# A fused two-layer transformer kernel: attention output, norm and first routing moved by batch into the stages around them

## The chip, the cores and the metric

The kernel runs on one core of a Trainium2 chip. The metric is the device time of one execution in microseconds (us), as the median of several executions. The core has five engines that run side by side: TensorE (PE) for matmuls and transposes, VectorE (DVE), ScalarE (ACT), GpSimd (POOL) and SyncE (SP), which here issues nearly all DMAs. They meet only through semaphores.

## The reference, cut to what matters

```
x = L0_attn_x                                   # 4 batches, 1024 tokens, width 128
x = x + attn(layernorm(x)) @ wo                 # 16 heads of 8, mask by pages of 32
xn = layernorm(x)
scores = softmax(xn @ gate_w.T)                 # 8 experts
weights, idx = top_k(scores, 2)
y = sum over e of (x2_e * x3_e * (idx == e))    # experts on xn * weight
x = x + y + silu(xn @ sw1.T) * (xn @ sw2.T) @ sw3.T
x = x + mamba(layernorm(x));  x = x + second_moe(layernorm(x))
```

The attention divides by its softmax sums, multiplies with `wo`, adds to x, normalizes, and a router picks two of eight experts for every token. That part, between the attention and the expert layer, is what the change moves.

## The kernel before, in words

The 4096 tokens are 8 chunks of 512, two to a batch. `X` stays in SBUF as [128 tokens, 32 tiles, 128]; `xnT` is its normalized transpose.

**Attention** (`attend`) runs 16 groups `i` of 4 heads; groups 0 to 3 are batch 0, and so on. A group has 9 steps `k`, a step two pairs. For a pair PE first computes one item of row maxima (`maxima`, L694) that lies 26 items ahead, then scores (L716), then values (L735) of an earlier step. DVE reduces the maxima (L622, 18 a group), ACT takes the exponentials (L670, 36 a group) and stores a group's output (`store`, L659), which SP writes to DRAM (`heads`, L539). POOL negates the next group's maxima (`negate`, L589 to L594); at step 7 PE turns them (`turn`, L702), ACT copies them, SP copies them into the rows of `qr` (L545), and the next group's scores wait for that DMA. SP also loads the rows of the group three ahead: 18 DMAs (L496, L491) at the start of each group up to the 13th. Maxima items end in group 14 (counted from 0), at its step 4. PSUM banks 0 to 3 hold maxima, 4 to 6 scores, 7 values.

**`attention_out`** loads numerators and inverse sums of 8 chunks (4 DMAs of 256 KB a batch, L816 and L817), divides on DVE (L841), multiplies with `wo` on PE (L878), adds to X and takes statistics on DVE (L846, L85). **`norm_transpose`** computes mean and 1/std (seven small DVE steps, POOL's power, L134), normalizes (DVE, L164), turns (PE, L177), copies (ACT, L209) and computes the router's logits (PE, L183). **`route_first`** does softmax and top two in 19 small dependent DVE steps over all 32 tiles at once, turns gates and masks, and writes them to DRAM.

**`first_ffn`** takes one chunk at a time, a Fori over 4 pairs of chunks. For expert e: SP broadcasts a gate row (L1020) and a mask row (L1023) into rings of four; POOL multiplies (`xm`, L1035, three ahead) and accumulates (L1046); PE does `up`, `third` and `second(e-1)`, two 512-column matmuls each (L1147, L1151, L1156); ACT the silu (L1059); DVE `x3s` (L1087) and `product(e-1)` (L1097). In the next chunk PE's `finish` (24 matmuls, L1138 and L1139) closes the chunk.

```
sp.wait_ge(xm_ready, q - ROW_RING + 1)          # before gate row q
pe.wait_ge(prod_ready, 2 + NE * c + e)          # second(e): product(e-1) is done
pe.wait_ge(exp_done, unit - 1)                  # scores: three banks, two written
```

Each stage is a block of its own: all engines meet at its end.

Of the kernel before, what the change touches and what calls it, by code (L numbers as in the profile page):

```python
# [9 lines left out]
F32 = mybir.dt.float32  # L10
BF16 = mybir.dt.bfloat16
# [4 lines left out]
P = 128  # L16
# [401 lines left out]
EARLY = (B - 1) * H  # L418
# [42 lines left out]
TURN_K = 7  # L461
PIECE = 256
# [37 lines left out]
def attend(nc, g):  # L500

    with ExitStack() as ctx:
# [13 lines left out]
        sums = sb("sums", [2 * EARLY, CH])  # L516
        zero_set, ones_set, bottom_set = sem("zero_set"), sem("ones_set"), sem("bottom_set")
        sums_in, inverted, inverse_out = sem("sums_in"), sem("inverted"), sem("inverse_out")
# [3 lines left out]
        out_written = [sem(f"out_written{k}") for k in range(2)]  # L522
# [13 lines left out]
        def _(sp):  # L536
# [15 lines left out]
            for i in range(NG):  # L552
                if i >= 1 and i + RING - 1 < NG:
                    sp.wait_ge(scores_done, UNITS * i)
                    for n in range(ROW_DMAS):
                        load_rows(sp, g, i + RING - 1, n)
                if i >= 1:
                    store(i - 1)
                if i == NG - 1:

                    for k in range(2):
                        sp.wait_ge(out_written[k], 16 * (EARLY // GH // 2))
                    sp.dma_start(sums[:, :], g.heads[0:EARLY, :, D, :]).then_inc(sums_in, 16)
                    sp.wait_ge(inverted, 1)
                    sp.dma_start(g.inverses[0:EARLY, :, :].rearrange("i a (k t) -> i (a k) t", k=CPB), sums[:, :]).then_inc(inverse_out, 16)
                else:
                    neg_in_rows(i + 1)
            store(NG - 1)
            for k in range(2):
                sp.wait_ge(out_written[k], 16 * NG // 2)  # L570
            sp.wait_ge(inverse_out, 16)

        @block.gpsimd
        def _(pool):
# [30 lines left out]
            for i in range(NG - 1):  # L605
                if i >= 1:
                    pool.wait_ge(values_done, NV * i)
                value_columns(i + 1)
                negate(i + 1)

        @block.vector
        def _(dve):
# [28 lines left out]
            dve.wait_ge(sums_in, 16)  # L641
            dve.reciprocal(sums[:, :], sums[:, :]).then_inc(inverted, 1)

        @block.scalar
        def _(act):
# [16 lines left out]
            for i in range(NG):  # L662
                for k in range(NK):
# [3 lines left out]
                    for h in range(GH):  # L667
# [6 lines left out]
                        if k == TURN_K and h == 0 and i < NG - 1:  # L674
                            turned(i + 1)
            store(NG - 1)

        @block.tensor
        def _(pe):
# [63 lines left out]
            for i in range(NG):  # L743
                for k in range(NK):
                    for pair in range(GP):
# [25 lines left out]
def top_two(eng, steps, s, rank, tmp, w1, mask):  # L771


    def over(t):
        return t.rearrange("p (n a) -> p n a", a=1).to_broadcast([P, NT, NE])
    ranks = rank.rearrange("p (a e) -> p a e", a=1).to_broadcast([P, NT, NE])
    steps.done(eng.tensor_reduce(w1[:, :], s[:, :, :], AX.X, ALU.max))
    steps.done(eng.tensor_tensor(tmp[:, :, :], s[:, :, :], over(w1[:, :]), ALU.is_equal))
    steps.done(eng.tensor_tensor(tmp[:, :, :], tmp[:, :, :], ranks, ALU.mult))
    steps.done(eng.tensor_reduce(w1[:, :], tmp[:, :, :], AX.X, ALU.max))  # L780
    steps.done(eng.tensor_tensor(mask[:, :, :], ranks, over(w1[:, :]), ALU.is_equal))

    steps.done(eng.scalar_tensor_tensor(tmp[:, :, :], mask[:, :, :], -4.0, s[:, :, :], ALU.mult, ALU.add))
    steps.done(eng.tensor_reduce(w1[:, :], tmp[:, :, :], AX.X, ALU.max))
    steps.done(eng.tensor_tensor(tmp[:, :, :], tmp[:, :, :], over(w1[:, :]), ALU.is_equal))
    steps.done(eng.tensor_tensor(tmp[:, :, :], tmp[:, :, :], ranks, ALU.mult))
    steps.done(eng.tensor_reduce(w1[:, :], tmp[:, :, :], AX.X, ALU.max))
    steps.done(eng.tensor_tensor(tmp[:, :, :], ranks, over(w1[:, :]), ALU.is_equal))
    steps.done(eng.tensor_tensor(mask[:, :, :], mask[:, :, :], tmp[:, :, :], ALU.add))


def attention_out(nc, g, e):

    with ExitStack() as ctx:
        sb = lambda name, shape, dt=F32: ctx.enter_context(nc.sbuf_tensor(f"ao_{name}", shape, dt))
        sem = lambda name: ctx.enter_context(nc.semaphore(f"ao_{name}"))
        X, PS = g.X, g.PS
        wo = sb("wo", [P, E])
        inverse = sb("inverse", [2 * H, CH])
        num, inv = sb("num", [P, 2, CH]), sb("inv", [P, 2, CH])  # L800
        headT = sb("headT", [P, 2, CH])
        w_in, sums_in, inverted, inverse_out, divided, added, mixed, stats_ready = map(sem, (
            "w_in", "sums_in", "inverted", "inverse_out", "divided", "added", "mixed", "stats_ready"))
        heads_in = [sem(f"heads_in{k}") for k in range(2)]
        block = ctx.enter_context(nc.Block())

        @block.sync
        def _(sp):
            sp.sem_inc(divided, 2)
            sp.dma_start(wo[:, :], g.w["wo"]).then_inc(w_in, 16)  # L810

            def load(b):
                for k in range(CPB):
                    sp.wait_ge(divided, CPB * b + k + 1)
                    heads, tokens = bass.ds(b * H, H), slice(k * CH, (k + 1) * CH)
                    sp.dma_start(num[:, k, :], g.heads[heads, k, 0:D, :]).then_inc(heads_in[k], 16)  # L816
                    sp.dma_start(inv[:, k, :], g.inverses[heads, :, tokens].to_broadcast([H, D, CH])).then_inc(heads_in[k], 16)  # L817

            load(0)
            sp.dma_start(inverse[:, :], g.heads[EARLY:, :, D, :]).then_inc(sums_in, 16)  # L820
            with sp.Fori(1, B - 1) as b:
                load(b)
            sp.wait_ge(inverse_out, 16)
            load(B - 1)
            for dst, src in e.pairs:
                sp.dma_start(dst, src).then_inc(e.loaded, 16)

        @block.scalar
        def _(act):
            for dst, src in e.route.pairs:  # L830
                act.dma_start(dst, src).then_inc(e.route.loaded, 16)
            act.wait_ge(inverted, 1)
            act.dma_start(g.inverses[EARLY:, :, :].rearrange("i a (k t) -> i (a k) t", k=CPB), inverse[:, :]).then_inc(inverse_out, 16)
        @block.vector
        def _(dve):
            dve.sem_inc(mixed, 2)

            def divide(b, k, c):
                dve.wait_ge(heads_in[k], 32 * (b + 1))
                dve.wait_ge(mixed, c + 1)  # L840
                dve.tensor_tensor(headT[:, k, :], num[:, k, :], inv[:, k, :], ALU.mult).then_inc(divided, 1)  # L841

            def add(c, k):
                dve.wait_ge(mixed, 2 + c + 1)
                x = X[:, bass.ds(c * TPC, TPC), :]
                dve.tensor_tensor(x, x, PS[:, k, :].rearrange("p (j e) -> p j e", e=E), ALU.add).then_inc(added, 1)  # L846

            def stats(c):
                dve.wait_ge(added, 2 + c + 1)
                for j in range(TPC):  # L850
                    last = tile_stats(dve, g, c * TPC + j)
                last.then_inc(stats_ready, 1)

            divide(0, 0, 0)
            divide(0, 1, 1)
            dve.wait_ge(sums_in, 16)
            dve.reciprocal(inverse[:, :], inverse[:, :]).then_inc(inverted, 1)
            with dve.Fori(0, B - 1) as b:
                for k in range(CPB):
                    add(CPB * b + k, k)  # L860
                    divide(b + 1, k, CPB * (b + 1) + k)
                    stats(CPB * b + k)
            for k in range(CPB):
                add(NCH - CPB + k, k)
                stats(NCH - CPB + k)
            dve.wait_ge(stats_ready, NCH)

        @block.tensor
        def _(pe):
            pe.wait_ge(w_in, 16)  # L870
            pe.sem_inc(added, 2)
            with pe.Fori(0, B) as b:
                for k in range(CPB):
                    c = CPB * b + k
                    pe.wait_ge(divided, 2 + c + 1)
                    pe.wait_ge(added, c + 1)
                    for j in range(TPC):
# [1114 lines left out]
```

## Time and profile before

| what | value |
|---|---|
| time of three runs | median 1487.25 us (1486.56 to 1489.18) |
| profiled execution | 1483.77 us, its span 1482.0 us |
| busy in the span | PE 82%, DVE 76%, ACT 45%, POOL 44% |
| granted TensorE clock, mean | 0.903 of full |
| attention, from the first exponential to the last | 125.4 to 473.0 us |
| from the last attention output copy to the first matmul of the expert layer | 474.2 to 546.1 us |
| expert layer, first matmul to last add | 546.1 to 772.0 us |

Times in rows count from the start of the span. Idle time of an engine matters only where it sets the end of a stage.

### The profile page before, as it was taken

The numbers are of one execution on the slowest core, as the hardware profiler recorded it, in microseconds if no ns is written. First come the engines' busy times: TensorE is split into PE (matmuls) and PEld (weight loads), VectorE is DVE, ScalarE is ACT, GpSimd is POOL, SyncE is SP. The second block draws the span as 40 slices with busy tenths as digits, with TensorE's granted clock in tenths as the row PEclk, the third lists the DMA queues.
The fourth block names the chain that finished last, engine by engine and source line by source line (L and its number), as shares of the span: only waits on it lengthen the run. The fifth ranks groups of instructions, "written<-read, shape, count | busy, mean of one in ns | idle before, by whom it ended". The sixth has DMA issues, their size and how long they took to land. (4 is left out here: it accounts for less than half of the span.)

```text
span 1482.0 us, 21932 instructions
## 1 busy us (share of the span) xinstructions
PE 1214.9 (82%) x7478; PEld 558.0 (38%) x7478; DVE 1132.8 (76%) x1294; ACT 669.5 (45%) x1046; POOL 645.6 (44%) x464
## 2 busy tenths in 40 slices
PE   4937999999996659999978767877877867766998
PEld 2412334334332544454444212322322322355565
DVE  5868999999990734545556889999999999964554
ACT  2515999999997022222225783333333323302221
POOL 2320000101010206766743068988989989921000
PEclk9956999999999559999997868999999999995999
DMA  4321111111101526334520013432333323400421
GB/s 105 120 94 43 58 49 50 61 47 54 54 17 43 157 40 134 127 106 119 121 51 18 5 52 128 127 128 103 115 122 128 128 98 118 125 8 26 68 57 43
DMA packets 74478, 120.31 MB, mean 81 GB/s; under 512 B 13150, under 2 KB 41638, under 8 KB 74390
## 3 DMA queue, kind: packets, MB, share of 16 engines
q1 hardware_dynamic: 74054, 119.08, 27.5%
q8 instruction: 53, 0.87, 0.2%
q14 instruction: 35, 0.29, 0.1%
q10 hardware_dynamic: 336, 0.07, 0.0%
HBM read 105.09 MB, written 13.63 MB: 80 GB/s over the span
## 5 line engine op out<-in xcount | busy, mean ns | idle before, releaser
L622 DVE TENSOR_REDUCE att_found<-PS 128x2 f32<-128x1024 f32 (+2 forms) x288 | 333.1, 1218 | 10.7 <-PE PS L694 8.8
L1518 PE MATMUL PS<-ms_ch,ident_sb 128*128 128x512 f32 x512 | 269.0, 651 | 72.4 <-POOL ms_ch L1625 72.4
L670 ACT ACTIVATE att_prob<-PS 128x512 f32<-128x512 f32 x576 | 313.4, 596 | 28.4 <-PE PS L716 15.3
L1625 POOL TENSOR_TENSOR ms_ch<-xnT,ms_c_rows 128x1024 f32<-128x1024 f32 x128 | 304.8, 2392 | 41.1 <-DVE xnT L1583 21.6
L1583 DVE TENSOR_TENSOR_SCAN xnT<-ms_decay,PS 128x1024 f32<-128x1024 f32 x96 | 216.0, 2275 | 4.2
L735 PE MATMUL PS<-att_prob,att_v 128*32 128x256 f32 (+1 forms) x2560 | 181.8, 370 | 3.0 <-ACT att_out L659 2.8
L1518 PEld LDWEIGHTS PS<-ms_ch,ident_sb 128*128 128x128 f32 x512 | 98.5, 203 | 194.6 <-POOL ms_ch L1625 107.5
L1556 ACT ACTIVATE PS<-m_dt,m_a 128x1024 f32<-128x1024 f32 x32 | 35.8, 1118 | 260.3 <-DVE xnT L1583 260.3
L694 PE MATMUL PS<-kr,qr 55*128 55x128 bf16 (+4 forms) x1152 | 120.8, 290 | 29.8 <-PEq L260 16.0
L716 PE MATMUL PS<-qr,kr 55*128 55x128 bf16 (+4 forms) x1152 | 114.1, 275 | 14.7 <-ACT att_prob L670 8.2
L1570 DVE TENSOR_TENSOR PS<-ms_dtu,PS 128x1024 f32<-128x1024 f32 x96 | 114.6, 1212 | 6.7 <-PE PS L1509 6.5
L1553 ACT ACTIVATE ms_decay<-m_dt,m_a 128x1024 f32<-128x1024 f32 x96 | 106.2, 1138 | 13.3 <-DVE xnT L1583 13.3
L1087 DVE SCALAR_TENSOR_TENSOR f_x3s<-PS,e_w_b,f_mask_row 128x512 f32<-128x512 f32 x64 | 48.0, 751 | 76.3 <-PE PS L1151 76.2
L1059 ACT ACTIVATE f_h<-PS,e_w_b 128x512 f32<-128x512 f32 x64 | 44.0, 687 | 132.3 <-PE PS L1147 132.3
L1035 POOL TENSOR_TENSOR f_xm<-xnT,f_gate_row 128x512 f32<-128x512 f32 x64 | 81.2, 1270 | 44.0 <-DMA f_gate_row<-gate_rows_dram 41.1
L1046 POOL TENSOR_TENSOR f_yT<-f_yT,f_prod 128x512 f32<-128x512 f32 x56 | 70.9, 1266 | 58.0 <-DVE f_prod L1097 55.5
L1509 PE MATMUL PS<-m_bc,m_w_sel_b 96*128 96x512 bf16 x192 | 63.9, 418 | 33.9 <-DVE xnT L1583 25.2
L694 PEld LDWEIGHTS PS<-kr,qr 48*128 48x128 bf16 (+1 forms) x1152 | 39.6, 97 | 135.5 <-issue 93.0
L134 POOL TENSOR_TENSOR norm_rstd<-norm_tmp,half 128x4 f32<-128x4 f32 x32 | 32.1, 1041 | 110.1 <-DVE norm_tmp L155 110.1
L599 POOL COPY att_v<-V 128x256 f32<-128x256 f32 x32 | 11.8, 398 | 156.3 <-PE PS L735 156.1
L735 PEld LDWEIGHTS PS<-att_prob,att_v 128*32 128x32 f32 x2560 | 54.7, 108 | 62.3 <-issue 53.6
L1632 POOL TENSOR_TENSOR ms_x_row<-ms_dtu,ms_b_row 128x1024 f32<-128x1024 f32 x32 | 75.1, 2348 | 1.8 <-DMA ms_b_row<-bc_rows_dram 1.8
(194 smaller groups left out, 1705.8 us busy)
## 6 DMA issues: line engine op xcount, KB each, us to landing
ms_c_rows<-bc_rows_dram SPq DMA_DIRECT2D x64, 512.0 KB, 5.9
f_gate_row<-gate_rows_dram SPq DMA_DIRECT2D x64, 256.0 KB, 3.5
ms_b_row<-bc_rows_dram SPq DMA_DIRECT2D x32, 512.0 KB, 3.6
f_mask_row<-mask_rows_dram SPq DMA_DIRECT2D x64, 128.0 KB, 3.1
qk_parts_dram<-qkv_parts SPq DMA_DIRECT2D x48, 128.0 KB, 1.8
heads_dram<-att_out SPq DMA_DIRECT2D x16, 256.0 KB, 2.6
f_mask_row<-mask_rows_dram SPq DMA_DIRECT2D x64, 64.0 KB, 3.3
qr<-qk_parts_dram SPq DMA_DIRECT2D x32, 96.0 KB
```

Of the source, the lines that this page charges most:

```text
L622: dve.tensor_reduce(found[:, :, pair, first:first + (n - 1) * step + 1:step], PS[:, bank:bank + 2, :].rearrange("p r (w n) -> p r w n", w= ...
L670: act.activation(prob[:, step % PROB_RING * GH + h, :], PS[:, SCORE_BANK + unit % SCORE_RING, :], ACT.Exp, scale=float(D) ** -0.5).then_in ...
L694: last = pe.matmul(PS[:, MAX_BANK + 2 * (m % 2) + r, at:at + n], rows(qr, count, i, pair, r, q_block * P, P), rows(kr, count, i, pair, r, ...
L716: last[r] = pe.matmul(PS[:, SCORE_BANK + (unit + r) % SCORE_RING, col:col + w], rows(kr, count, i, pair, r, j * P, P), rows(qr, count, i, ...
L735: last = pe.matmul(PS[VW * h:VW * (h + 1), VALUE_BANK, q - half * CH:q - half * CH + w], v1[:, i % 2, half, h, j, :], prob[:, step % PROB_ ...
L1035: pool.tensor_tensor(xm[:, e % XM_RING, :], xnT[:, c * CH:(c + 1) * CH], gate_row[:, e % ROW_RING, :], ALU.mult).then_inc(xm_ready, 1)
L1518: last = pe.matmul(PS[:, Y_BANK + 2 * half + q, :], g.ident[:, :], ch[:, half, q * CH:(q + 1) * CH], start=j == 0 and not odd, stop=j == J ...
L1553: act.activation(decay[:, 2 * odd + half, :], m.dt[:, half, sequence(b)], ACT.Exp, scale=m.a[:, half, n + odd:n + odd + 1]).then_inc(decay ...
L1570: dve.tensor_tensor(inputs(half), dtu[:, half, :], inputs(half), ALU.mult).then_inc(input_ready, 1)
L1583: dve.tensor_tensor_scan(h[:, odd, half, :], factor, x, 0.0, ALU.mult, ALU.add).then_inc(scanned, 1)
L1625: pool.tensor_tensor(ch[:, half, :], h[:, odd, half, :], c_rows[:, s % C_RING, :], ALU.mult).then_inc(ch_ready, 1)
L1632: pool.tensor_tensor(x_row[:, :], dtu[:, 1, :], b_row[:, :], ALU.mult).then_inc(x_row_ready, 1)
```

## The change

The blocks `attention_out`, the norm in front of the expert layer and `route_first` disappear. A class `Front` holds their work as small pieces with fixed places, for each batch b of 1024 tokens.

```
LOADS_AT = 6
SUMS_AT, INVERT_AT, INVERSES_AT, HEADS_AT = (5, 9, 13), (8, 12), (8, 12), (10, 14)

# SP, attention group i
+                if i == LOADS_AT:
+                    sp.dma_start(f.wo[:, :], g.w["wo"]).then_inc(f.wo_in, 16)
+                    for group in (f.e.route, f.e):
+                        for dst, src in group.pairs:
+                            sp.dma_start(dst, src).then_inc(group.loaded, 16)
...
+                for b in range(EARLY):
+                    if i == INVERSES_AT[b]:
+                        f.store_inverses(sp, b)
+                    if i == HEADS_AT[b]:
+                        f.load_heads(sp, b)
# POOL, after value_columns(i + 1) and negate(i + 1)
+                for b in range(EARLY):
+                    if i + 1 == HEADS_AT[b]:
+                        for k in range(CPB):
+                            f.divide(pool, b, k)
+            for b in range(EARLY):
+                f.root(pool, b)
# DVE, before the maxima item m
+                for b in range(EARLY):
+                    if m == NI * INVERT_AT[b]:
+                        f.invert(dve, b)
# ACT, after step k
+                    if i == NG - 1 and k in (0, 4):
+                        for part in range(CPB):
+                            f.store_x(act, k // 4, part)
+                    if i == NG - 1 and k in (2, 6):
+                        f.exp(act, k // 4)
+                    if i == NG - 1 and k == 7:
+                        f.store_rows(act, 0)
# PE, after step k
+                    if i == NG - 2 and k in (6, 7):
+                        pe.wait_ge(max_taken, NG * NI)
+                        for part in range(CPB):
+                            f.mix(pe, k - 6, part)
+                    if (i, k) == (NG - 2, 8) or (i, k) == (NG - 1, 3):
+                        for part in range(CPB):
+                            f.turn_x(pe, k // 8 ^ 1, part)
+                    if i == NG - 1 and k in (1, 5):
+                        f.logits(pe, k // 4)
+                    if i == NG - 1 and k == 6:
+                        f.turn_rows(pe, 0)
...
+            f.turn_rows(pe, 1)
```

After its last maxima item DVE does `invert(2)`, then for batch 0 `add` (with statistics), `moments` (seven steps), `normalize`, for batch 1 `add`, and so on to the 19 routing steps of each batch. In the expert layer, now written out for all 8 chunks instead of a loop, batches 2 and 3 are placed at pairs (chunk, expert):

```
# SP: after the mask row of (0, 3): load_heads(2), load_sums(3); (1, 1) store_inverses(3); (1, 4) load_heads(3)
#     (3, 7) store_row_tables(2); (6, 0) store_row_tables(3)
# POOL, at the end of the turn of e (which begins with gated(e + 3)):
+                    if c == 0 and e in (1, 2):
+                        f.divide(pool, 2, e - 1)
+                    if (c, e) == (0, 6):
+                        f.root(pool, 2)
# PE, after second(e - 1)
+                    for b, at, part in ((2, (0, 3), 0), (2, (0, 4), 1), (3, (2, 7), 0), (3, (3, 1), 1)):
+                        if (c, e) == at:
+                            f.mix(pe, b, part)
+                    for b, at, part in ((2, (1, 1), 0), (2, (1, 2), 1), (3, (3, 5), 0), (3, (3, 6), 1)):
+                        if (c, e) == at:
+                            f.turn_x(pe, b, part)
# DVE, after product(e - 1)
+                for b, at, part in ((2, (0, 7), 0), (2, (1, 1), 1), (3, (3, 5), 0), (3, (3, 6), 1)):
+                    if (c, e) == at:
+                        f.normalize(dve, b, part)
# ACT
+                    for b, at in ((2, (1, 6)), (3, (4, 3))):
+                        if (c, e) == at:
+                            act.preload_act_table(ACT.Exp)
+                            f.exp(act, b)
+                            act.preload_act_table(ACT.Silu)
```

The other pieces of batches 2 and 3 are placed in the same way (DVE: `invert(3)` at (0, 2), `add(2)` at (0, 4) and (0, 5), `moments(2)` at (0, 6); PE: `logits` at (1, 4) and (4, 1), `turn_rows` at (2, 7) and (5, 2)). Two of the new functions:

```
    def load_heads(self, sp, b):
        sp.wait_ge(self.inverse_out, 16 * (b + 1))
        if b > 0:
            sp.wait_ge(self.divided, CPB * b)
        for k in range(CPB):
            sp.dma_start(self.num[:, k, :], ...).then_inc(self.heads_in[k], 16)
            sp.dma_start(self.inv[:, k, :], ...).then_inc(self.heads_in[k], 16)

    def divide(self, pool, b, k):
        pool.wait_ge(self.heads_in[k], 32 * (b + 1))
        ...
        pool.tensor_tensor(self.headT[...], self.num[:, k, :], self.inv[:, k, :], ALU.mult).then_inc(self.divided, 1)
```

The division moves from DVE to POOL. A chunk's `mix` or `turn_x` is four fp32 products of 128 columns, 8 matmul instructions; a batch's `logits` is 16.

## Rows read from the trace of the kernel before

**Rows 1.** Stretches: length; busy PE, PEld, DVE, ACT, POOL; clock, DMA share, GB/s.
```profile
441.00:475.00 34.00, 28.33 (x413) 10.38 (x409) 5.47 (x5) 31.26 (x59) 1.25 (x5) 1.00 0.07 22
...
508.00:532.00 24.00, 20.17 (x96) 19.64 (x96) 9.30 (x35) 4.79 (x10) 8.10 (x8) 0.50 0.00 1
...
602.00:658.00 56.00, 55.83 (x166) 27.18 (x165) 30.13 (x48) 13.98 (x21) 38.96 (x32) 1.00 0.38 117
```

**Rows 2.** Timeline, both ends of the gap: start, length, engine, line, operation, idle before.
```profile
474.18 0.60 ACT L659 ACTIVATE att_out<-PS 128x512 f32<-128x512 f32 x1 [1.20 <-PE PS L735]
...
546.08 2.04 PE L1147 MATMUL PS<-xnT,e_w_sw 128*128 128x512 f32 x2 [3.50 <-PEq L1125]
```

**Rows 3.** Timeline, end of group 14.
```profile
448.55 1.46 SPq L545 DMA_DIRECT2D qr<-att_neg_rows  x2
...
452.03 0.14 PEld L716 LDWEIGHTS PS<-qr,kr 55*128 55x128 bf16 x4 [0.66 <-DMA qr<-att_neg_rows]
```

**Rows 4.** Timeline, first `finish`: its first matmul, and the first one behind it.
```profile
580.73 0.61 PE L1138 MATMUL PS<-e_w_sw,f_hid 128*128 128x128 f32 x4
...
583.41 1.02 PE L1147 MATMUL PS<-f_xm,e_w_w 128*128 128x512 f32 x2
```

**Rows 5.** Timeline, 485 to 537 us: the small operations that move.
```profile
485.21 3.33 DVE L857 RECIPROCAL ao_inverse<-ao_inverse 32x512 f32<-32x512 f32 x1
...
503.10 0.67 DVE L846 TENSOR_TENSOR X<-X,PS 128x512 f32<-128x512 f32 x1
...
504.64 0.69 DVE L846 TENSOR_TENSOR X<-X,PS 128x512 f32<-128x512 f32 x1
...
506.86 0.21 DVE L149 TENSOR_TENSOR norm_tmp<-stats 128x32 f32<-128x32 f32 x1 [0.62 <-PEq L794]
...
508.53 8.10 POOL L134 TENSOR_TENSOR norm_rstd<-norm_tmp,half 128x4 f32<-128x4 f32 x8 [63.73 <-DVE norm_tmp L155]
509.92 2.28 DVE L164 TENSOR_SCALAR norm_xn<-X,norm_mean,norm_rstd 128x128 f32 x8 [1.47 <-POOL norm_rstd L134]
...
536.49 0.42 DVE L780 TENSOR_REDUCE r_w<-r_tmp 128x32 f32<-128x256 f32 x1
```

**Rows 6.** Timeline, group 10: store of group 9, negation, turn, copy into the rows.
```profile
356.31 0.38 SPq L539 DMA_DIRECT2D heads_dram<-att_out  x1
...
357.06 0.25 POOL L589 TENSOR_TENSOR att_neg<-att_zero,att_row_max 128x32 f32<-128x32 f32 x1 [8.21 <-DVE att_row_max L635]
...
362.10 0.26 PE L702 MATMUL PS<-identb_sb,att_neg_parts 128*96 128x128 bf16 x1
...
362.75 1.55 SPq L545 DMA_DIRECT2D qr<-att_neg_rows  x2
```

**Rows 7.** Timeline, `attention_out`: loads of a batch, its divisions, loads of weights.
```profile
477.78 0.67 SPq L816 DMA_DIRECT2D ao_num<-heads_dram  x1
...
482.36 0.69 DVE L841 TENSOR_TENSOR ao_headT<-ao_num,ao_inv 128x512 f32<-128x512 f32 x1 [18.93 <-DMA ao_inv<-inverses_dram]
...
484.60 0.69 DVE L841 TENSOR_TENSOR ao_headT<-ao_num,ao_inv 128x512 f32<-128x512 f32 x1 [1.54 <-DMA ao_inv<-inverses_dram]
...
499.99 2.19 SPq L826 DMA_DIRECT2D e_w_sw<-sw  x3
```

**Rows 8.** Stretches of 1 us, PE alone: busy, granted clock, DMA share, GB/s.
```profile
477.00:478.00 1.00, 0.00 (x0) 0.71 0.00 0
...
549.00:550.00 1.00, 0.53 (x1) 0.95 0.73 133
```

**Rows 9.** Timeline, expert layer's first chunk: a gate row's DMA, its reader.
```profile
550.91 1.36 SPq L1020 DMA_DIRECT2D f_gate_row<-gate_rows_dram  x1
...
561.20 1.26 POOL L1035 TENSOR_TENSOR f_xm<-xnT,f_gate_row 128x512 f32<-128x512 f32 x1 [2.17 <-DMA f_gate_row<-gate_rows_dram]
```

**Rows 10.** Timeline, routing: a table load on ACT and the exponential behind it.
```profile
532.00 1.28 ACT L925 ACT_TABLE_LOAD   x1 [3.02 <-PEq L96]
...
533.29 0.42 ACT L927 ACTIVATE r_s<-r_tmp 128x256 f32<-128x256 f32 x1
```

More of the change, by code:

```diff
@@ L639, in _ @@
                     dve.wait_ge(row_max_ready, m // NI)
+                for b in range(EARLY):
+                    if m == NI * INVERT_AT[b]:
+                        f.invert(dve, b)
                 take(m)
-            dve.wait_ge(sums_in, 16)
-            dve.reciprocal(sums[:, :], sums[:, :]).then_inc(inverted, 1)
+            f.invert(dve, 2)
+            for k in range(CPB):
+                f.add(dve, 0, k)
+            f.moments(dve, 0)
+            for k in range(CPB):
+                f.normalize(dve, 0, k)
+            for k in range(CPB):
+                f.add(dve, 1, k)
+            f.route_scores(dve, 0)
+            f.moments(dve, 1)
+            for k in range(CPB):
+                f.normalize(dve, 1, k)
+            f.route_weights(dve, 0)
+            f.route_first(dve, 0)
+            f.route_second(dve, 0)
+            f.route_rows(dve, 0)
+            f.route_scores(dve, 1)
+            f.route_weights(dve, 1)
+            f.route_first(dve, 1)
+            f.route_second(dve, 1)
+            f.route_rows(dve, 1)
         @block.scalar
@@ L768 @@
 XM_AHEAD = 3
[L771 to L789, printed above, removed]
@@ L792, in attention_out @@
[L792 to L877, printed above, removed]
-                        last = pe.matmul(PS[:, k, j * P:(j + 1) * P], headT[:, k, j * P:(j + 1) * P], wo[:, :], start=True, stop=True)
-                    last.then_inc(mixed, 1)
@@ new lines, in first_of_two @@
+def first_of_two(eng, steps, s, rank, tmp, w1, mask):
+    tiles = s.shape[1]
+    over = lambda t: t.rearrange("p (n a) -> p n a", a=1).to_broadcast([P, tiles, NE])
+    ranks = rank.rearrange("p (a e) -> p a e", a=1).to_broadcast([P, tiles, NE])
+    steps.done(eng.tensor_reduce(w1, s, AX.X, ALU.max))
+    steps.done(eng.tensor_tensor(tmp, s, over(w1), ALU.is_equal))
+    steps.done(eng.tensor_tensor(tmp, tmp, ranks, ALU.mult))
+    steps.done(eng.tensor_reduce(w1, tmp, AX.X, ALU.max))
+    steps.done(eng.tensor_tensor(mask, ranks, over(w1), ALU.is_equal))
@@ new lines, in second_of_two @@
+def second_of_two(eng, steps, s, rank, tmp, w1, mask):
+    tiles = s.shape[1]
+    over = lambda t: t.rearrange("p (n a) -> p n a", a=1).to_broadcast([P, tiles, NE])
+    ranks = rank.rearrange("p (a e) -> p a e", a=1).to_broadcast([P, tiles, NE])
+    steps.done(eng.scalar_tensor_tensor(tmp, mask, -4.0, s, ALU.mult, ALU.add))
+    steps.done(eng.tensor_reduce(w1, tmp, AX.X, ALU.max))
+    steps.done(eng.tensor_tensor(tmp, tmp, over(w1), ALU.is_equal))
+    steps.done(eng.tensor_tensor(tmp, tmp, ranks, ALU.mult))
+    steps.done(eng.tensor_reduce(w1, tmp, AX.X, ALU.max))
+    steps.done(eng.tensor_tensor(tmp, ranks, over(w1), ALU.is_equal))
+    steps.done(eng.tensor_tensor(mask, mask, tmp, ALU.add))
@@ L1023, in _ @@
                     sp.dma_start(mask_row[:, r, :], g.mask_rows[0, e:e + 1, tokens].to_broadcast([P, CH])).then_inc(mask_in[r], 16)
+                    if (c, e) == (0, 3):
+                        f.load_heads(sp, 2)
+                        f.load_sums(sp, 3)
+                    if (c, e) == (1, 1):
+                        f.store_inverses(sp, 3)
+                    if (c, e) == (1, 4):
+                        f.load_heads(sp, 3)
         @block.gpsimd
@@ L1046, in _ @@
                         pool.tensor_tensor(yT[:, c % 2, :], yT[:, c % 2, :], prod[:, e % 2, :], ALU.add).then_inc(summed, 1)
+                    if c == 0 and e in (1, 2):
+                        f.divide(pool, 2, e - 1)
+                    if (c, e) == (0, 6):
+                        f.root(pool, 2)
+                    if c == 1 and e in (3, 4):
+                        f.divide(pool, 3, e - 3)
+                    if (c, e) == (3, 2):
+                        f.root(pool, 3)
         @block.scalar
```

321 lines of the change are left out of this document (232 added, 89 removed).

## The prediction

> **What bounds the kernel now.** I read the profile in this order. The timeline at the stage edges shows the target: the attention's last copy starts at 474.2, the expert layer's first matmul at 546.1 [rows 2], 71.9 us in which no main stage runs. The stretches then tell what the three places that take the work in have to spare. Late attention (441 to 475): ACT is busy 31.3 of 34 us, PE 28.3 [rows 1]; PE is handed a bank when an exponential ends and must refill it before the next, so its 5.7 us of idle lie in some 29 crumbs of 0.2 us. The expert layer past its first chunk: PE is busy 55.8 of 56 us for two chunks [rows 1], with nothing spare; DVE (30) and POOL (39) have room. Its first chunk is different: `xm(4)` starts only 15.1 us in, and its gate row took from 550.9 to 561.2 to arrive [rows 9]; there the row DMAs are the bound. So the work does not vanish: most of PE's share lands on an engine that is full, now at full clock.
>
> **What goes.** All 71.9 us, three stage edges and two half-clock stretches with it (clock 0.50 with PE busy 20.2 of 24 us [rows 1]).
>
> **What comes back in the attention before its last two groups.**
> (a) Two reciprocals on DVE, which sets the pace there. 512 wide takes 3.33 us [rows 5], so 128 wide is 0.83, plus hand-over 0.95: 1.9 us. Bounds 0 and 2.
> (b) Group 6: SP issues 12 more DMAs (2 MB) between the row loads and the store of group 5. Three issues take 2.19 us [rows 7], so 12 take 7 to 9. In this pattern (group 10 shows it) 6.1 us lie between the end of that store's issue and the copy into `qr` [rows 6], and scores follow that copy's issue by 3.5 us [rows 3], just in time. SP is 1 to 3 us late and the copy queues behind 2 MB: 2.5 us (0 to 5).
> (c) Group 10: POOL, having negated for group 10, goes to `divide(0)` and waits for SP's `load_heads(0)`, issued after the store, at 356.7 in the old clock [rows 6]. Queued behind this wait are `value_columns(11)` and `negate(11)`; PE's turn waits for the latter, then everything. From the first load's issue to the first division took 4.6 us, to the second 6.8 [rows 7]: divisions on POOL (1.27 us, like the multiply in [rows 9]) at 361.3 and 363.5, two copies 0.7, five small negation steps 1.6: negation ends at 367.2 instead of 358.6, and the turn at 362.1 [rows 6] becomes 367.4. That is 5.3 us, 5.0 after buffers. Bounds 2 and 7. For batch 1 the same order costs nothing: no row loads run in group 14 and the heads land some 7 us before the negation is due.
> (d) Such a pause can drop the clock: PE's last work ended near 474.1, and the clock fell within 477 to 478; it rose again in the fourth microsecond after work began [rows 8]. Half speed for 3 us costs about 1.2 (0 to 3).
> Together 10.6 us.
>
> **What comes back in the last two groups.** 24 small matmuls take 583.41 - 580.73 = 2.68 us, 0.112 each [rows 4], so a 16-matmul piece is 1.8 us. Mix, turn and logits for two batches are six pieces, plus two row turns: 11.2. Crumbs give back 1.5. ACT adds four copies (0.6 each, like [rows 2]), two exponentials, four small copies: 3.5, at other steps than PE's pieces, so added. Waits: after `mix(0)`, DVE needs two adds with statistics (1.54 each, the two adds of [rows 5]), seven moment steps of 0.2 to 0.24 (1.5), POOL's root, and 0.28 x 4 = 1.15 a chunk to normalize. Root: 128x4 takes 1.01 [rows 5]; 128x8 lies between 1.0 and 2.0; I take 1.9, since plain POOL steps on 128x32 take 0.25 [rows 6], so the power's price goes by columns. This chain ends 0.7 us after PE asks for `turn_x(0)`; with the second chunk, and the same for batch 1, 1.7. Routing has 17 steps after the exponential, each between 0.21 (32 wide) and 0.42 (256 wide) [rows 5], 0.27 with hand-over at 64 wide: 4.6; batch 1's ends just before the last values. The last row turn, two copies and two DMA issues stick out by 1.5. Sum 11.2 - 1.5 + 3.5 + 1.7 + 1.5 = 16.4 (12 to 24). Then the one stage edge that stays, 2.0.
>
> The layer now starts at 474.8 + 16.4 + 2.0 + 10.6 = 503.8 instead of 546.1: 42.3 gained.
>
> **What comes back in the expert layer.**
> (e) First chunk. `load_heads(2)` and `load_sums(3)` enter a saturated queue before gate row 4. A 256 KB DMA is issued there in 1.4 to 1.6 us [rows 9]: `xm(4)` slips by 6.5 (3.5 to 7.5) to 21.6. POOL does `gated(4)` and a sum before `divide(2, 0)`, although the heads came ahead of gate row 4: 21.6 + 1.3 + 1.25 + 1.27 = 25.4. PE, done with expert 3 at about 15.8, sits at `mix(2, 0)` until then; 9.6 us idle. `divide(2, 1)` ends at 29.2, again awaited. The second chunk would start at 40.5 instead of 31.2: 9.3 us (4 to 13).
> (f) DVE's `normalize(2, 0)` waits for the root, POOL's `root(2)` stands behind the sum for product 6; queued on DVE are product 7 and the shared product, for which PE's third(1) of the next chunk waits: 1.8 (0.5 to 3).
> (g) The 9.6 us pause drops the clock as in (d): 1.6 (0 to 2).
> (h) PE's pieces from chunk 1 on, five of 1.8 and two row turns: 9.5 (8 to 11).
> (i) `turn_x(3)` stands at the same pair as its `normalize` on DVE, at (3, 5) and (3, 6). DVE ends a pair 0.85 us after PE, then normalizes in 1.15: PE waits 2.1 twice, 4.2 (2 to 5).
> (j) Other DVE pieces (0.6 to 1.95) fit: DVE idles 0.9 us of a pair's 2.55 and product(e-1) has 0.85 to spare before PE's next second. ACT's two table loads of 1.28 and an exponential [rows 10] hold it 2.9 against 2.5 spare. I take 1.3 for all of these (0 to 6).
> Sum 27.7.
>
> On (j) the Trainium skill (ScalarE: Activation LUTs, What ACT_TABLE_LOAD costs) says that a switch of table sets also pays a drain of about 1.38 us, 2.66 in all. Here the exponential starts 1.29 us after the load does [rows 10], so no drain behind the load shows. By the page four loads would hold ACT 5.5 us longer; the estimate from it would be some 5 us more in the sum, and the row decides.
>
> **Sum.** 1483.8 (the profiled execution's own time) - 42.3 + 27.7 = 1469.2. That execution is 3.5 below the median of the runs shown, so I forecast 1472.7, rounded 1472.5, 14.7 us faster.
>
> **The rivals.**
> *Stalls mostly hidden.* If heads and rows overlap better, (c), (e), (f), (i) shrink to their low ends, 3.0 + 5.3 + 1.3 + 2.2 less, and the waits in the last groups vanish, 2: 13.8 less, about 1459. For it: SP's copies usually land in time. Against it: POOL's order in (c) and (e) is fixed by code.
> *More waits, still faster.* The upper ends lie 26.3 us above the values taken, all together (7.6 of it in the last two groups); with a fifth to two fifths of that, 1478 to 1484. For it: nearly each piece joins three in-order engines.
> *The change moves nothing in the end* (no gain, within 0.2%): PE's waits in (c), (e), (i), 18.5 in the sum, are 1.8 times as long. 1487.
> *Slower: the clock falls in the attention's end and stays.* From 508 to 532 PE was busy 84% with just these transposes and logits, at 0.50 [rows 1]. PE's work from 441 on, 28.3 + 11.2 = 39.5 us at full clock, would take 79 at half. Against it: there the scores and values between the pieces run at 1.00 all along. Price for the whole stretch +30: 1502; it decides the sign from about 15 us of PE work at half clock on, half the stretch.
>
> **Chances.** Forecast (1464 to 1478) 0.55; hidden stalls (below 1464) 0.20; more waits (1478 to 1484) 0.12; no gain 0.04; slower 0.09. A measurement here can tell 0.2%, 3 us: faster 0.87, same 0.04, slower 0.09. Range 1458 to 1482: it takes in the two neighbours down to their middle and leaves out about 0.2.
>
> **What the profile after would show.** Layer's first matmul at 500 to 508. In group 10 PE idle for 5 us before it turns the negated maxima, and POOL idle until the heads land. Idle of 9 to 10 us before `mix(2, 0)`, ended by POOL's divide, the clock at 0.5 after it. Two idles of 2 us before `turn_x(3)`, ended by DVE. The expert layer 253 us long instead of 226. Wrong would be: heads late by more than 7 us in group 10, the clock at 0.5 in the last 30 us of the attention, or ACT as releaser of PE in the expert layer.

## The result, and the profile after

The changed kernel takes 1484.29 us (median of 20 executions, 1478.63 to 1488.58), the kernel before 1486.61 (20 executions, 1484.08 to 1491.93): a ratio of 0.9981, with a 95% interval of 0.9972 to 0.9990. That is 2.3 to 2.8 us less, a fifth of the 14.7 forecast, and outside the range 1458 to 1482.

The profiled execution took 1482.99 us, 13.8 more than the 1469.2 of the sum. First the place where the attention hands over, in the trace after (start, length, engine, line, operation, idle before), the last copy on ACT and the first matmul of the expert layer on PE:

```profile
494.56 0.60 ACT L694 ACTIVATE att_out<-PS 128x512 f32<-128x512 f32 x1 [1.20 <-PE PS L779]
...
498.38 2.05 PE L1311 MATMUL PS<-xnT,e_w_sw 128*128 128x512 f32 x2 [3.64 <-PEq L1289]
```

The layer starts at 498.4, where it started at 546.1 [rows 2]: 47.7 us gained, 5.4 more than the 42.3 forecast. What is lost comes later. These are the eight chunks of the expert layer on PE, after (length, busy, granted clock as a share of full speed, DMA share, GB/s):

```profile
498.38:543.22 44.84, 34.65 (x73) 0.77 0.55 138
543.22:574.14 30.92, 30.71 (x105) 0.97 0.45 135
574.14:605.62 31.48, 28.19 (x90) 1.00 0.31 101
605.62:650.63 45.01, 34.01 (x98) 0.85 0.23 71
650.63:682.62 31.99, 29.36 (x97) 0.98 0.31 100
682.62:710.94 28.32, 28.14 (x83) 0.96 0.40 112
710.94:738.06 27.12, 26.95 (x81) 1.00 0.49 102
738.06:769.86 31.80, 30.03 (x105) 1.00 0.30 56
```

and the same of before, the first three chunks:

```profile
546.08:577.29 31.21, 27.82 (x56) 0.95 0.88 158
577.29:604.33 27.04, 26.98 (x81) 1.00 0.36 115
604.33:631.37 27.04, 26.98 (x82) 1.00 0.37 117
```

Before, every chunk but the first and the last takes 27.0 us and the layer 225.2 (546.1 to 771.3). After, it takes 271.5. Against before the chunks lose 13.6, 3.9, 4.4, 18.0, 5.0, 1.3, 0.1 and 0.0 us, 46.3 together, where 27.7 were forecast. Chunk 3 alone loses 18.0. Of the 46.3 us, 22.3 are busy time of PE (242.0 us at a mean clock of 0.93, against 219.7 at 0.99), and 24.0 are idle time (29.4 against 5.5). PE's waits in the layer, after (who waits, for whom: us, times, longest):

```profile
PE PS L1320 <- DVE f_prod L1260: 10.8, 10, 2.6
PE PS L1012 <- DVE fr_xn L957: 9.4, 2, 5.4
PE PS L1005 <- POOL fr_headT L918: 6.5, 1, 6.5
```

The last row is the wait before `mix(2, 0)`, the middle one the two waits before `turn_x(3, .)`. The first, PE's waits for DVE's products, had only the 1.8 us of (f) and a part of the 1.3 of (j) in the forecast. Now DVE and POOL side by side in chunk 3, at DVE's `moments(3)`, first DVE:

```profile
618.75 0.16 DVE L943 TENSOR_TENSOR fr_moments_tmp<-stats 128x8 f32<-128x8 f32 x1
618.95 0.17 DVE L944 TENSOR_TENSOR fr_moments_tmp<-stats 128x8 f32<-128x8 f32 x1
619.15 1.13 DVE L945 TENSOR_TENSOR fr_moments_tmp<-stats 128x8 f32<-128x8 f32 x1
620.32 1.18 DVE L946 SCALAR_TENSOR_TENSOR fr_moments_tmp<-fr_moments_tmp 128x8 f32<-128x8 f32 x1
621.53 0.17 DVE L947 SCALAR_TENSOR_TENSOR fr_moments_tmp<-fr_moments_tmp 128x8 f32<-128x8 f32 x1
```

and POOL in the same stretch:

```profile
618.98 1.27 POOL L1162 TENSOR_TENSOR f_yT<-f_yT,f_prod 128x512 f32<-128x512 f32 x1 [8.34 <-DVE f_prod L1260]
620.22 1.25 POOL L1151 TENSOR_TENSOR f_xm<-xnT,f_gate_row 128x512 f32<-128x512 f32 x1
```

The reader is to see that `L943` and `L945` are alike, 8 columns from two operands in SBUF, and take 0.16 and 1.13 us. The long one starts inside POOL's add (618.98 + 1.27 = 620.25) and ends at 620.28; the next starts inside POOL's multiply (ends 621.47) and ends at 621.50. When POOL is idle again, 0.17 is back. So it goes with the normalizing steps, four to a group, at (1, 1) with POOL idle and at (3, 5) and (3, 6) with POOL at work:

```profile
554.00 1.11 DVE L957 TENSOR_SCALAR fr_xn<-X,fr_mean,fr_rstd 128x128 f32<-128x128 f32 x4
...
628.18 4.59 DVE L957 TENSOR_SCALAR fr_xn<-X,fr_mean,fr_rstd 128x128 f32<-128x128 f32 x4
...
638.90 3.05 DVE L957 TENSOR_SCALAR fr_xn<-X,fr_mean,fr_rstd 128x128 f32<-128x128 f32 x4
```

The 1.11 agrees with the 1.15 that the forecast took from [rows 5]. POOL was at work there as well, but with other steps: eight powers of 128x4, back to back from 508.53 to 516.63, and the eight normalizing steps beside them took 2.28 us together. So not every step of POOL holds DVE; the ones seen to do it here are its multiplies and adds, 512 or 256 columns wide. Beside the 4.59 POOL's 512-wide steps stand nearly back to back (626.54, 627.76, 628.98, 630.20, 631.42, each 1.26 long). The Trainium skill has a rule for it (SBUF — State Buffer, Who interferes with whom): a VectorE instruction with two inputs in SBUF, or one in a two-port mode such as `tensor_scalar` can enter, shares a port pair with GpSimd; whoever starts first has it for the whole instruction and the other blocks. The trace agrees for POOL's 512-wide steps, with the ends that coincide to 0.03 us, and steps with one input in SBUF and one in PSUM (`L1250`) keep 0.75; for the power steps of [rows 5] the blocking does not show.

### The profile page after: what moved, and what is told of

It is laid out like the page before. It is cut to its first block and busy times, and to the rows that moved or that the text cites. A ratio compares the mean times of both kernels' runs of the same rounds, so it can differ in the third digit from the quotient of the medians.

```text
span 1481.1 us, 21354 instructions
## 1 busy us (share of the span) xinstructions
PE 1214.6 (82%) x7478; PEld 548.8 (37%) x7478; DVE 1153.7 (78%) x1366; ACT 672.6 (45%) x1057; POOL 653.5 (44%) x468
## 5 line engine op out<-in xcount | busy, mean ns | idle before, releaser
L1250 DVE SCALAR_TENSOR_TENSOR f_x3s<-PS,e_w_b,f_mask_row 128x512 f32<-128x512 f32 x64 | 47.9, 749 | 75.3 <-PE PS L1315 73.7
L738 PEld LDWEIGHTS PS<-kr,qr 48*128 48x128 bf16 (+1 forms) x1152 | 39.7, 97 | 137.7 <-issue 89.5
L1320 PE MATMUL PS<-f_h,e_w_w 128*128 128x512 f32 x128 | 66.9, 605 | 10.8 <-DVE f_prod L1260 10.8
L1759 DVE TENSOR_TENSOR_SCAN xnT<-PS,ms_x_row 128x1024 f32<-128x1024 f32 x32 | 72.5, 2266 | 0.0
```

What stands on the lines that cost most here:

```text
L738: last = pe.matmul(PS[:, MAX_BANK + 2 * (m % 2) + r, at:at + n], rows(qr, count, i, pair, r, q_block * P, P), rows(kr, count, i, pair, r, ...
L1759: dve.tensor_tensor_scan(h[:, odd, half, :], factor, x, 0.0, ALU.mult, ALU.add).then_inc(scanned, 1)
```

## The experiments

Each was timed beside the kernel before, on the same chip: runs 1 to 8 on one, 9 to 11 on a second, 12 on a third. Ratios are to the kernel before. Differences to the changed kernel are to its median of 1484.29, which was not timed again beside them (the kernel before had medians from 1486.5 to 1488.8), so they hold to about 2 us. Lengths of chunks and waits are from one profiled execution each. Unless a diff says otherwise, each starts from the changed kernel.

**One edit each: three waits of place.** Run 1, PE's turn and ACT's copies of batch 3 one expert later:

```
-  turn_x(pe):     (3, (3, 5), 0), (3, (3, 6), 1)
+  turn_x(pe):     (3, (3, 6), 0), (3, (3, 7), 1)
-  store_x(act):   (3, (3, 6), 0), (3, (3, 7), 1)
+  store_x(act):   (3, (3, 7), 0), (3, (4, 0), 1)
```

> One edit of the changed kernel: PE turns the two normalized chunks of batch 3 one expert later, at (3, 6) and (3, 7) instead of (3, 5) and (3, 6), and ACT copies them one expert later too; DVE normalizes at the same places as in the changed kernel. Theory A, only the place of the turn is wrong (PE waits 9.4 us for DVE and the clock falls after it): both waits go and most of the low clock, 8 to 12 us less than the changed kernel's 1484.3, about 1474. Theory B, DVE itself is held up there, because its normalizing steps take 4.59 and 3.05 us beside POOL's multiplies instead of 1.11: DVE is late with the products all the same and PE waits for these instead; 3 to 6 us less, about 1480, with PE's waits for products longer than 10.8 us. Theory C, the clock falls by itself from PE's small transposes: 0 to 2 us less.

1475.15 us, ratio 0.9922 (0.9899 to 0.9946): 9.1 less than the changed kernel. Chunk 3 takes 35.0 us instead of 45.0, and PE's waits are:

```profile
PE PS L1320 <- DVE f_prod L1260: 10.7, 9, 2.6
...
PE PS L1012 <- DVE fr_xn L957: 2.1, 1, 2.1
```

Theory A holds as far as the time goes: the waits for products did not grow, they stayed at 10.7. The normalizing steps are as long as before (mean 735 ns), but one expert of distance hides most of it. One wait of 2.1 is left, where theory A had both go. Theory C falls.

Run 2, POOL divides batch 0 after it has negated for group 11:

```
+  DIVIDE_AT = (11, 14)
-  if i + 1 == HEADS_AT[b]:  divide(b, 0), divide(b, 1)
+  if i + 1 == DIVIDE_AT[b]: divide(b, 0), divide(b, 1)
```

> One edit of the changed kernel: POOL divides the heads of batch 0 after it has negated the maxima of group 11, not before it; the loads stay in group 10. The prediction's term (c) puts 5 us there: PE's idle of 4.4 us before it turns the negated maxima goes, and the time falls by 4 to 6 us, to about 1479.5. Rival: the row copies of group 10, issued behind the heads, are as late as the negation, and only 0 to 2 us come back.

1476.82 us, ratio 0.9939 (0.9919 to 0.9959): 7.5 less. The layer's first matmul comes at 491.4 instead of 498.4. PE's wait of 4.4 us before it turns the negated maxima is gone, and so is a fall of the clock behind it: in the changed kernel PE ran at 0.73 and 0.58 in 365 to 370 and 370 to 375, here at 1.00 in both. This is more than the 4 to 6 expected, which left out the clock: the group takes 4.5 us less than in the changed kernel and the next one 2.2 less.

Run 3, the heads of batch 2 loaded by SP right after `store_inverses(2)`, in its idle time from 472 on, and divided at the end of POOL's attention part; run 4, the same with DVE's reciprocal of batch 3 at (0, 4) instead of (0, 2):

```
   f.store_inverses(sp, 2)
+  f.load_heads(sp, 2)
...
   for b in range(EARLY): f.root(pool, b)
+  for k in range(CPB): f.divide(pool, 2, k)
...
-  load_heads(sp, 2) at (0, 3);  divide(pool, 2, .) at (0, 1), (0, 2)
```

> Of the changed kernel, the heads and inverses of batch 2 are loaded by SP in the attention's last group (SP is idle there from 472 to 491) and divided by POOL at the attention's end; nothing of it is left in the first chunk, where load_sums(3) alone stays ahead of gate row 4. Theory A, the prediction's term (e): the idle of PE before mix(2, 0) and the late gate rows go with the 1 MB of loads: 7 to 11 us less than 1484.3, about 1475. Theory B, DVE's reciprocal of batch 3, which waits 4.6 us for its sums in the same place, holds the chunk up as well: 2 to 5 us less. Theory C, the gate rows' own queue bounds the first chunk: 0 to 2 us less.

> As the run before (heads of batch 2 early), and DVE takes the reciprocal of batch 3 at expert 4 of the first chunk instead of expert 2. If the wait for the sums counts once the heads are out of the way: 2 to 4 us less than the run before. If the sums, now at the head of the queue, land in time: within 1 us of it.

Run 3: 1476.71 us, ratio 0.9939 (0.9919 to 0.9959), 7.6 less; the first chunk falls from 44.8 to 36.3 us. Run 4: 1474.74 us, ratio 0.9927 (0.9903 to 0.9951), not to be told from run 3, and its first chunk takes 36.2. DVE's wait of 4.6 us for the sums, which the forecast had not seen, is gone in the trace of run 3 already: with no heads in front of them the sums land in time, and the second edit has nothing left to remove. That is the second branch of what was expected.

**The contention.** Run 5 cuts POOL's two standing steps in the changed kernel, run 6 does so in the kernel before, and run 12 cuts them by half only:

```
-  xm[:, r, :]    = xnT[:, chunk] * gate_row[:, r, :]
+  xm[:, r, 0:16] = xnT[:, first 16 of chunk] * gate_row[:, r, 0:16]     (run 12: 256)
-  yT[:, k, :]    += prod[:, e % 2, :]
+  yT[:, k, 0:16] += prod[:, e % 2, 0:16]                                (run 12: 256)
```

> The changed kernel with POOL's two standing steps of the first expert layer, the multiply that gates an expert's input and the add of its product, cut from 512 to 16 columns (most of the gating and of the sum over experts is left out; all waits and signals stay). POOL's steps fall from 1.26 us to about 0.1 to 0.2. Theory A, DVE's small steps are stretched by POOL's 512-wide steps: normalize falls from a mean of 734 ns to 345, L945, L946, L833, L834, L846, L847 from 1.0 to 1.3 us to 0.2; PE's waits for normalized chunks fall from 9.4 to 3 to 5 us and for products from 10.8 to under 4; the kernel falls by 10 to 16 us more than the kernel before does under the same cut. Theory B, those steps are long for a reason of their own: they stay long and the difference between the two kernels stays within 3 us of 2.3.

> The kernel before with the same cut of POOL's two steps in the first expert layer from 512 to 16 columns (most of the gating and of the sum is left out). PE is full there in the kernel before: 0 to 4 us less (the waits for gated inputs of the first chunk, 3.1 us, and for the last sum, 1.6). It is the base for the run before.

> The changed kernel with POOL's two standing steps of the first expert layer cut to 256 columns, half their width (half of the gating and of the sum is left out); POOL's steps should take about 0.7 us. If a DVE step that meets a POOL step lasts until that one ends: L945, L946, L834 and L847, which take 1.13 to 1.19 us beside steps of 1.26, take 0.6 to 0.7 (not 0.2 and not 1.2), the mean of normalize lies near 500 ns, between 342 (16 columns) and 734 (512), and the time between 1458.8 and 1484.3, some 12 us below the changed kernel. If the stretch had another source, the steps would keep 1.1 to 1.3 us.

Run 5: 1458.81 us, ratio 0.9813 (0.9797 to 0.9828), 25.5 less than the changed kernel. Run 6: 1484.03, ratio 0.9982 (0.9972 to 0.9992), 2.6 to 2.9 less than the kernel before. The layer takes 247.4 us in run 5 (501.5 to 748.9) and 223.8 in run 6. With POOL out of the way the move costs it 23.6 us, against 46.3 with POOL's steps at full width. The rows of DVE, run 5 (busy, mean ns):

```profile
L957 DVE TENSOR_SCALAR fr_xn<-X,fr_mean,fr_rstd 128x128 f32<-128x128 f32 x16 | 4.4, 342 | 2.0 <-POOL fr_rstd L922 2.0
L834 DVE TENSOR_TENSOR fr_tmp<-fr_tmp,r_w_rank 128x64 f32<-128x64 f32 x2 | 0.4, 224 | 0.1
L945 DVE TENSOR_TENSOR fr_moments_tmp<-stats 128x8 f32<-128x8 f32 x2 | 0.3, 173 | 0.1
L946 DVE SCALAR_TENSOR_TENSOR fr_moments_tmp<-fr_moments_tmp 128x8 f32<-128x8 f32 x2 | 0.3, 167 | 0.1
```

run 12, where POOL's steps take 728 ns:

```profile
L957 DVE TENSOR_SCALAR fr_xn<-X,fr_mean,fr_rstd 128x128 f32<-128x128 f32 x16 | 6.6, 471 | 2.5 <-POOL fr_rstd L922 2.5
L946 DVE SCALAR_TENSOR_TENSOR fr_moments_tmp<-fr_moments_tmp 128x8 f32<-128x8 f32 x2 | 1.3, 648 | 0.1
L945 DVE TENSOR_TENSOR fr_moments_tmp<-stats 128x8 f32<-128x8 f32 x2 | 1.2, 588 | 0.1
```

and the changed kernel, 1260 ns:

```profile
L957 DVE TENSOR_SCALAR fr_xn<-X,fr_mean,fr_rstd 128x128 f32<-128x128 f32 x16 | 10.8, 734 | 3.0 <-POOL fr_rstd L922 3.0
L834 DVE TENSOR_TENSOR fr_tmp<-fr_tmp,r_w_rank 128x64 f32<-128x64 f32 x2 | 2.4, 1189 | 0.1
L946 DVE SCALAR_TENSOR_TENSOR fr_moments_tmp<-fr_moments_tmp 128x8 f32<-128x8 f32 x2 | 2.4, 1180 | 0.1
L945 DVE TENSOR_TENSOR fr_moments_tmp<-stats 128x8 f32<-128x8 f32 x2 | 2.3, 1130 | 0.1
```

The same DVE instruction takes 0.17, 0.65 and 1.18 us as POOL's step takes 0.22, 0.73 and 1.26. Run 12's time, 1469.93 (0.9886, 0.9867 to 0.9904), lies in between as well, 14 us below the changed kernel where 12 were expected. A DVE step that meets one of these POOL steps waits for its end; theory B of run 5 falls. In run 5 PE's waits are 1.7 us for products (10.8 in the changed kernel) and 3.9 before the two turns (9.4). One caution: the cut also makes POOL's own results earlier. That this is the smaller part shows in PE's waits for POOL's results, which go from 9.2 to 8.1 us in the layer (the one before `mix(2, 0)` from 6.5 to 5.3), while its waits for DVE's results go from 20.2 to 6.5. The rest of the gain is PE's busy time, 232.7 us at a clock of 0.97 instead of 242.0 at 0.93. The time fell by some 23 us more than the kernel before did under the same cut, where theory A had 10 to 16; PE's shorter busy time is a part that it did not name.

Run 7 leaves the work where it was and only writes the loops out, a rival for the excess:

```
-  with eng.Fori(0, NCH // 2 - 1) as i: chunk(2 * i + 1, ...); chunk(2 * i + 2, ...)
+  for c in range(NCH): chunk(c, c % 2, c > 0)
```

> The kernel before with the loops over the first expert layer's chunks written out for PE, DVE and ACT, as the change does besides its move of work, and nothing else. If the loops cost or hide nothing: within 2 us of the kernel before. If writing them out is part of what the change lost (instructions fetched only once each): 4 to 10 us slower.

1488.44 us, ratio 1.0016 (1.0006 to 1.0027): 1.5 to 2.4 slower. The layer takes 226.1 instead of 225.2 us. Written-out loops are 0.9 of the 18.6 us by which the layer missed its forecast.

**Together.** Run 8 has the edits of runs 1 to 4. Run 9 adds ACT as the one that normalizes batches 2 and 3, run 10 also POOL as the one that computes their moments, and run 11 is run 8 with POOL's steps cut as in run 5:

```
   # run 9, from run 8
+  down = -mean * rstd                                              (DVE, one step a batch)
-  dve.tensor_scalar(xn, X, mean, rstd, subtract, mult)
+  act.activation(xn, X, Identity, bias=down, scale=rstd)
   # run 10, from run 9
-  f.moments(dve, b)
+  f.moments_pool(pool, b)                                          (in front of root(b))
```

> The changed kernel with the edits of the runs so far together: turn of batch 3 one expert later, division of batch 0 after the negation of group 11, heads of batch 2 loaded and divided early, reciprocal of batch 3 two experts later. If the waits are independent: 9.2 + 7.5 + 9.6 = 26 us less than 1484.3, about 1458. If ACT, or the attention's own pace, takes part of it back: 15 to 20 less.

> The kernel with all four edits, and ACT normalizes the chunks of batches 2 and 3 (one activation a tile, with scale and bias from a small step of DVE) instead of DVE. Theory A, the rest of the excess sits where DVE's steps meet POOL's: the eight stretched normalizing steps (10.8 us of DVE in the expert layer) leave DVE, PE's 3.2 us of waits before the turns and DVE's wait for the root go: 3 to 5 us less than 1461.2. Rival: ACT, with some 1.2 us more a chunk, holds PE up instead, or the wait for the root moves to ACT: 0 to 2 us less, or slower.

> As the run before, and POOL computes the moments of batches 2 and 3 itself (eight steps of 8 columns, right before its root) instead of DVE. DVE's two or three moment steps that last 1.13 to 1.20 us beside POOL's go, and with them PE's waits for products of 3.4 and 1.5 us at (0, 6) and (3, 2): 3 to 5 us less than the run before if the theory of the shared port holds; within 1 us of it, or slower, if POOL's own steps (eight of 0.1 to 0.25 us and the root) make its gated inputs late instead.

> The kernel with all four edits and POOL's two standing steps of the first expert layer cut from 512 to 16 columns (most of the gating and of the sum is left out). It tells how much of the contention is left once the placed waits are gone. If the four edits took away only waits of place and the stretched steps still cost: 8 to 14 us less than 1461.2 (PE's waits for products go from 11.5 to under 3). If most of the 22.6 us that the same cut gave in the changed kernel came through the very waits that the edits removed: 3 to 8 us less.

Run 8: 1461.16 us, ratio 0.9825 (0.9806 to 0.9845), 25.8 less than before and 23.1 less than the changed kernel: 3 short of the 26 of independent waits, and more than the 15 to 20 of the rival. Its first chunk takes 35.3 us and chunk 3 34.7. Run 9: 1462.74 (0.9815, 0.9796 to 0.9834). Run 10: 1457.26 (0.9819, 0.9796 to 0.9842). The intervals of the three overlap, and their layers take 251.4, 250.0 and 251.1 us: neither step adds anything that can be measured. (Run 10's median is 5.5 us below run 9's, but its executions spread from 1456 to 1466 us and the ratios agree.) In run 9 the waits before the turns are gone, but PE's waits for products stay at 11.4. In run 10 these fall to 6.8, and a new one of 4.2 comes, since DVE now waits 6.4 us for the root:

```profile
PE PS L1349 <- DVE f_prod L1289: 6.8, 8, 2.6
PE PS L1344 <- DVE f_hid L1297: 4.2, 1, 4.2
```

So run 9 went by its rival, 0 to 2 us less or slower, and for run 10 the 3 to 5 us are not shown: what PE gains on the products it loses on the root. Run 11: 1440.70 (0.9704, 0.9675 to 0.9733), 20.5 less than run 8, or 18 by the ratios, since the two ran on different chips. Its layer takes 231.4 us, PE waits 1.3 us for products, and the first chunks are:

```profile
492.49:523.21 30.72, 29.71 (x72) 0.89 0.61 162
523.21:553.11 29.90, 29.73 (x105) 1.00 0.49 143
553.11:580.93 27.82, 27.82 (x90) 1.00 0.34 116
580.93:609.42 28.49, 28.49 (x98) 1.00 0.39 112
```

This beat the expectation of 8 to 14. With no wait of place and no stretched step, all the moved work costs the layer 231.4 - 223.8 = 7.6 us over run 6; PE is busy 228.5 us against 219.5 there, both at a clock of 0.99, so its pieces take 9.1, and it idles 1.5 less. What the contention leaves on PE in run 8 are the waits for products, 11.5 us at the places where DVE does moments and routing, 2.0 for the shared product (`f_hid`), and 3.2 before the turns.

## Why the prediction was wrong

By its own steps, against the trace after.

*The attention before its last two groups, forecast 10.6 us.* The copy into `qr` of group 14 is issued at 435.6 instead of 427.3, 8.3 later, and 9.0 counted from the same start of the attention (0.8 us earlier here). (a) DVE takes the reciprocals before the first maxima items of groups 8 and 12, and these items lie 26 ahead of the scores: in the trace the reciprocals stand at 270.21 and 357.81, in groups 6 and 10. Each is followed by a wait of PE that the kernel before does not have, this one in group 10:

```profile
PE PS L738 <- DVE att_found L635: 0.7, 1, 0.7
```

In run 2, where the division no longer stands in group 10, the group still takes 22.4 us against 21.6 before. So a reciprocal costs 0.8, both 1.6, and 1.9 were put. (b) Group 6 and the one behind it cost 1.5 with the reciprocal, so the loads cost some 0.7, forecast 2.5. (c) and (d) are the mechanism forecast. POOL's negation for group 11 ended at 368.0 (forecast 367.2), PE turned at 368.2 after this wait:

```profile
367.78 0.24 POOL L601 TENSOR_TENSOR att_neg_parts<-att_neg_rest,att_neg_parts 128x32 bf16<-128x32 f32 x1
...
368.17 0.31 PE L746 MATMUL PS<-identb_sb,att_neg_parts 128*96 128x128 bf16 x1 [4.40 <-POOL att_neg_parts L601]
```

The group took 5.3 us more, of which 0.8 are the reciprocal and 4.5 are (c), forecast 5.0; the next one took 2.2 more at the lower clock, which is (d), forecast 1.2. Run 2 took both back.

*The last two groups, forecast 16.4.* From the copy for group 14 to the end of the attention's last copy: before 427.3 to 474.8, after 435.6 to 495.2, so 12.1 more. PE lost only 0.7 us to the turns where 1.7 were put, and the pieces fit into ACT's pace better than by sum. The edge to the layer is 3.2 us, forecast 2.0. The slower rival, a clock that falls here, was partly right: in the last group PE runs at 0.70 for 5 us (473.6 to 478.6). From the copy for group 15 to the layer's first matmul the traces of runs 1 to 4 and 10 show 39.7 to 39.8 us, as the changed kernel's does, and the others with the changed attention (5, 8, 9, 11, 12) 40.9 to 45.1, with a longer stretch at the lower clock. That moves some microseconds between traces, not the sign.

*The expert layer, forecast 27.7, measured 46.3.* Here is the error. The steps (e), (f) and (g), 12.7 for the first chunk, come near: it is 13.6 us longer. That is in part luck, since the parts differ. PE's wait before `mix(2, 0)` is 6.5, not 9.6, the clock falls to 0.5 behind it as forecast, the root cost 3.0 us of DVE, and PE waits 2.6 us for a product behind two stretched moment steps. PE also starts the layer at a lower clock than before, 0.50 and then 0.60 over its first 10 us (before: 0.69, then 1.00), which no step had. Runs 3 and 4 take 8.5 us of it back, and run 11 all of it (30.7 against the 31.2 of before). (h) PE's pieces, forecast 9.5, take 9.1 by the busy times of runs 11 and 6.

The steps that failed are (i) and (j), which took DVE's steps at lengths that hold only away from POOL's wide steps, and the clock behind the waits, which (g) priced at 1.6 us for one pause and no step priced for the others. In (i) the place and the mechanism were right ("DVE ends a pair 0.85 us after PE, then normalizes in 1.15: PE waits 2.1 twice"), but the 1.15 came from a row where POOL ran only its short power steps [rows 5]. Beside POOL's 512-wide steps it is 4.59 and 3.05, and PE waits 5.45 and 3.91, with the clock at 0.66 on average from 628 to 648. In run 5, with short POOL steps, PE waits 3.9 in both together: the forecast's 4.2. Chunk 3 loses 18.0 us; moving the turn gives 10.0 of it back, cutting POOL's steps gives 10.0 as well. In (j), "Other DVE pieces (0.6 to 1.95) fit", the slack of 0.85 us was judged against the same undisturbed lengths. `route_first` takes 3.3 us (586.4 to 589.7) instead of 1.2, `moments` 3.4 instead of 1.5, and PE waits 10.8 us in ten places. The clock: PE's busy time in the layer grew by 22.3 us, and its pieces are 9.1 of that, so by this estimate some 13 us are the lower clock (0.93 on average instead of 0.99). ACT's table loads, the worry of the forecast, cost nothing that shows: two pairs of 1.28 us in the layer, the exponential 1.29 us behind the start of its load (567.77 and 569.06), and no matmul of PE waits for ACT there.

The sum then reads: 1469.2 - 5.4 (attention and edge) + 18.6 (expert layer) + 0.6 (behind it and around it) = 1483.0. Of the layer's 46.3 us, 46.3 - 23.6 = 22.7 go with POOL's full-width steps. The -5.4 helped: without the last two groups, put 4.3 us too high, the time would have missed by that much more. It is shown that DVE's steps wait for POOL's wide ones (ends that coincide, and three widths). That those 22.7 us are this alone is not shown to the microsecond, since the cut makes POOL faster too. What a kernel that still computes the right result could get back of run 8's 11.5 us of waits for products, say with DVE's small steps in POOL's idle time, was not tried.

## What to carry to other kernels

The length of an instruction is a row of its neighbourhood. When VectorE work is moved from a stretch where GpSimd is idle to one where it is busy, each step with two SBUF operands, and `tensor_scalar` from SBUF to SBUF, is to be priced at up to the length of the wide GpSimd step beside it (here 1.2 us instead of 0.2); many small steps suffer most. A row of the same instruction gives its length only if the same kind of GpSimd step ran beside it. And a wait of TensorE has a second price, the clock behind it: here some 13 us beside 24 of idle time. And in an engine that works in order, the reader of a moved piece belongs one whole turn behind its writer: here the turn and the division moved back by one place, and one batch's loads moved ahead, were worth 23 us, ten times what the change itself gave.

## What the runs showed of the hardware that was not expected

- A VectorE step of 8 or 64 columns with two SBUF operands that meets a 256 or 512 columns wide multiply or add of GpSimd lasts until that one ends: 0.17 us (8 columns) and 0.22 (64) alone, 0.65 beside steps of 0.73, 1.18 beside steps of 1.26. An f32 `tensor_scalar` of 128 columns goes from 0.34 us on average to 0.47 and 0.73.
- GpSimd's power steps do not do this: in the kernel before all 128 normalizing steps take 0.34 to 0.35 us, also those beside eight powers of about 1.01 us each [rows 5].
- Steps with a single SBUF input are not held: in the changed kernel a reduction (`L845`, 596.33) takes 0.22 us and a reciprocal (`L979`, 672.61) 0.20 in the middle of a POOL step, and steps with one operand in PSUM and one in SBUF (`L1250`) take 0.749 us for 512 columns with POOL's steps at 512 as at 16.
- The clock falls behind waits of this size. Waits of PE of 5.5 and 3.9 us in chunk 3 were each followed by a stretch at the lower of the two levels (1.2 GHz): the mean granted clock was 0.66 from 628 to 648, with PE busy 11.3 of 20 us. In run 1, with one wait of 2.1, chunk 3 as a whole ran at 0.95 instead of 0.85. How long it lasts varies: runs 3 and 4 have the same two waits, 9.4 us together, and chunk 3 ran at 0.85 in one (45.8 us) and at 0.92 in the other (42.1).
- In the attention's last group, whose code on PE, ACT and DVE is the same in all traces with the changed attention, the lower clock lasted for different lengths, worth up to 5 us. Each trace is one execution of another kernel, so it is not shown what decides it.
